# Selection products for the second attention's head stacks, key copies on ScalarE, and a new order of GpSimd's and SyncE's work

## The chip, the cores and the metric

The kernel runs on 1 core of one Trainium2 chip. The metric is the device time of one execution in microseconds (us). Engines are TensorE (PE in rows; PEld is its weight load), VectorE (DVE), ScalarE (ACT), GpSimd (POOL) and SyncE (SP), which issues DMAs.

## What is computed

Two transformer layers on x, 2 batches of 512 tokens by 128 features, with a context of 2 x 154 tokens. `_layernorm` has no weights.

```python
x = x + L0_xattn(_layernorm(x), ctx)   # linear attention with elu+1 features, then its own layer norm
x = x + L0_ffn(_layernorm(x))          # gated recurrence over the 2 batches as steps, tanh output
x = x + L1_xattn(_layernorm(x), ctx)   # softmax attention, 16 heads of 8 features, padding mask
x = x + L1_ffn(_layernorm(x))          # 8 experts, top 2, hidden 256
# L1_xattn:
Q = (q @ Wq + bq).reshape(Bc, Tq, H, HD).transpose(0, 2, 1, 3)
KV = (kv @ Wkv + bkv).reshape(Bc, Tk, 2, H, HD).transpose(2, 0, 3, 1, 4)
attn = softmax(where(mask, -inf, einsum('bhqd,bhkd->bhqk', Q, K) * HD ** -0.5))
out = einsum('bhqk,bhkd->bhqd', attn, V)   # then @ Wo + bo
```

## The kernel before

All data stay in SBUF; each engine runs one program in order, and the engines wait for one another by semaphores. Product accuracy near float32 comes from splitting an operand in a high part (type fp32r) and a low part, the rest after it.

**Layer 0** (to about 60 us). Context keys and values (L804, L808), layer norm of x on VectorE and ScalarE (`ln_apply`, `normalise`), turned by TensorE; queries (L820), key-value state (L827), `numerator(b)` (L833) and, after VectorE's `quotient(b)`, `project(b)` (L838), then VectorE's `residual(b)` (L1214) with its statistics. GpSimd computes the reciprocal roots (`rstd_of`, L467). The gates of the second layer part are L871 to L885, with tanh on ScalarE (L685).

**Second attention.** The 16 heads go in `HQ` = 4 stacks of `HG` = 4 heads for each batch, 8 stacks `m` in all. A stack's 97 score rows are three blocks of `QB` = 32 rows (4 heads x 8 features) and a row for the mask. For the keys block 0 and 1 are the high part and block 2 the low; for the queries block 0 and 2 high and block 1 low, so one product of 97 rows holds high x high, low x high and high x low. Before the change GpSimd builds for this the repeated weights `wq_r`, `wk_r` and the repeated identity `ident_r` (`three_blocks`, L485 to L490). The product with repeated weights (L861 for keys, L907 for queries, both float32, two passes) lays the stack out in PSUM three times; ScalarE copies all blocks rounded to fp32r (L671, L701); VectorE overwrites the low block with the rest (L1257, L1288). Biases are turned into the same layout (L854). GpSimd then writes the keys four times, for each head with the other heads' rows times 0 (`kz`, `kz_t`, L541 and L543).

For stack `m` TensorE makes 8 score products (`scores`, L919), VectorE takes the negated row maxima of each (L1298) and splits them in three bf16 parts (L1306 to L1309), TensorE turns them (`max_turn`, L928) and ScalarE copies them under the queries (L597). Then 5 units for each stack: transposed scores `st(u)` (L950), exp (L722) and, `LAG` = 4 units later, the product with the values (`pv`, L967 and L970). `ITEMS` (L383) is the order, written by hand, in which turns, queries, scores and maxima are put between units; `PER_UNIT` says how many go behind each, `ALONE` how many go before the first unit, and each item takes the next of a ring of PSUM banks (`BEFORE` waits for its last user).

**Experts** (from about 160 us): products of high and low parts of weights and activations. ScalarE rounds the weights (`weight_hi`, L604, 8 instructions) and GpSimd computes the rest (`weight_lo`, L478, 8 instructions); GpSimd also subtracts the first row of each expert's weights (L515) and builds the expert selectors `pick_e` (L556, L557) and the parts of the bias (L560 to L563).

SyncE issues the loads x, row constants, the weights of layer 0, of its gates, of layer 1, then the experts' three loads of 1 MB; ScalarE issues the context, its weights, the column constants and the mask (L590 to L593).

## Time and profile before

| | |
|---|---|
| time, median of 3 runs | 227.08 us (225.4 to 227.48) |
| the profiled execution | 226.56 us |
| its span, first to last instruction | 224.8 us |
| TensorE busy | 172.1 us (77%) |
| VectorE busy | 143.8 us (64%) |
| ScalarE busy | 99.9 us (44%) |
| GpSimd busy | 81.0 us (36%) |
| mean granted TensorE clock | 0.863 of full |

The profile is of one execution. Times in a timeline are us from the span's start. A line is `start, duration, engine, source line, operation, out<-in, shapes, count` and in brackets the engine's idle time before and what ended it.
### The profile page before, as it was taken

To read this page: it belongs to the slowest core of one execution; us is meant where nothing else is said; L and a number is where in the kernel's file an instruction comes from. 1 tells how busy PE (TensorE), PEld (TensorE's weight loads), DVE (VectorE), ACT (ScalarE), POOL (GpSimd) and SP (SyncE) were. 2 spreads that over 40 slices of the span, in tenths; PEclk is the share of its full clock that TensorE was granted. 3 is DMA by queue.
4 is the path that set the end of the run, shared out by engine and by line. 5 is a ranking of instruction groups with operands and counts; after the bars stand their busy time and mean duration, and the time that the engine had idled before them with its cause. 6 is when DMAs were issued, how large, how long until landed. Compare 5 with 4: busy or idle time off the path is not lost.

```text
span 224.8 us, 2308 instructions
## 1 busy us (share of the span) xinstructions
PE 172.1 (77%) x663; PEld 101.0 (45%) x663; DVE 143.8 (64%) x422; ACT 99.9 (44%) x184; POOL 81.0 (36%) x101
## 2 busy tenths in 40 slices
PE   0558983199518709889696978876899998999994
PEld 0334471144114207444244364433467674767682
DVE  5596899845386898756517375553468695656651
ACT  2135773551415105565424335652554635464551
POOL 7399453679149970000000000110334423342420
PEclk9995579679985755999766788996999999999999
DMA  6995000000000000000000000000000000000101
GB/s 188 315 274 180 1 0 1 0 4 0 0 1 0 0 0 0 0 0 0 3 0 0 0 0 0 4 0 0 0 3 0 1 0 0 3 0 0 47 1 47
DMA packets 4560, 6.04 MB, mean 27 GB/s; under 512 B 412, under 2 KB 3268, under 8 KB 4548
## 3 DMA queue, kind: packets, MB, share of 16 engines
q1 hardware_dynamic: 3984, 5.47, 7.9%
q10 hardware_dynamic: 564, 0.43, 0.7%
q8 instruction: 5, 0.08, 0.1%
q14 instruction: 7, 0.06, 0.1%
HBM read 5.37 MB, written 0.52 MB: 26 GB/s over the span
## 4 chain that ended last, share of the span: by engine, by line
PE 49%; DVE 35%; ACT 7%; issue 4%; DMA 3%; POOL 0%; ACTq 0%; DVEq 0%
DVE nmax L1298 6%; PE bank L967 4%; PE bank L907 4%; DVE stats L1111 3%; PE bank L871 3%; PE bank L919 3%; PE bank L1055 3%; DVE nm_part L1306 3%; DMA wc_s<-in_w_ctx 3%; PE bank L797 3%; PE bank L970 3%; PE bank L950 2%; PE bank L1057 2%; PE bank L1056 2%; PE bank L1040 2%
## 5 line engine op out<-in xcount | busy, mean ns | idle before, releaser
L467 POOL TENSOR_TENSOR rstd<-vare,m_half 128x4 f32<-128x4 f32 x10 | 10.9, 1092 | 80.6 <-DVE vare L1116 80.1
L569 POOL TENSOR_TENSOR pair<-early,pair 128x512 fp32r<-128x512 f32 x16 | 20.5, 1283 | 42.9 <-ACT pair L747 42.9
L1298 DVE TENSOR_REDUCE nmax<-bank 128x2 f32<-128x308 f32 x64 | 27.1, 471 | 12.0 <-PE bank L919 11.4
L1386 DVE SCALAR_TENSOR_TENSOR pair<-bank,pair 128x512 fp32r<-128x512 f32 x32 | 21.6, 689 | 19.6 <-ACT pair L754 19.5
L722 ACT ACTIVATE prob<-bank 128x512 f32<-128x512 f32 x40 | 23.4, 597 | 22.2 <-PE bank L950 21.9
L919 PE MATMUL bank<-pair,q_s 97*128 97x308 f32 x64 | 24.2, 441 | 5.9 <-DVE q_s L1288 3.7
L919 PEld LDWEIGHTS bank<-pair,q_s 97*128 97x128 f32 x64 | 13.8, 226 | 20.5 <-issue 7.1
L747 ACT ACTIVATE pair<-early 128x512 fp32r<-128x512 f32 x16 | 10.1, 632 | 23.9 <-DVE early L1382 23.9
L950 PE MATMUL bank<-q_s,pair 112*128 112x512 f32 x40 | 20.7, 530 | 0.0
L754 ACT ACTIVATE pair<-bank 128x512 fp32r<-128x512 f32 x32 | 18.7, 594 | 4.3 <-PE bank L1042 3.1
L797 PE MATMUL bank<-ident,a_n 128*128 128x128 f32 x40 | 8.5, 350 | 13.1 <-DVE a_n L1122 13.0
L797 PEld LDWEIGHTS bank<-ident,a_n 128*128 128x128 f32 x40 | 6.3, 182 | 18.3 <-issue 15.6
L1055 PE MATMUL bank<-pair,w_h 128*128 128x512 f32 x32 | 14.1, 441 | 0.0
L1040 PE MATMUL bank<-pair,w_h 128*128 128x512 f32 x32 | 13.5, 421 | 0.0
L1288 DVE SCALAR_TENSOR_TENSOR q_s<-bank,bias_q,q_s 32x512 fp32r<-32x512 f32 x8 | 6.0, 744 | 10.6 <-ACT q_s L701 10.5
L1042 PE MATMUL bank<-pair,w_l 128*128 128x512 f32 x32 | 12.7, 396 | 0.0
L1041 PE MATMUL bank<-pair,w_h 128*128 128x512 f32 x32 | 12.7, 396 | 0.0
L1057 PE MATMUL bank<-pair,w_h 128*128 128x512 f32 x32 | 12.7, 396 | 0.0
L1056 PE MATMUL bank<-pair,w_l 128*128 128x512 f32 x32 | 12.6, 395 | 0.0
L1382 DVE TENSOR_TENSOR early<-bank,q 128x512 f32<-128x512 f32 x16 | 10.9, 683 | 1.4 <-PE bank L1026 1.3
L701 ACT ACTIVATE q_s<-bank,bias_q 97x512 fp32r<-97x512 f32 x8 | 5.5, 688 | 13.8 <-PE bank L907 13.8
L907 PE MATMUL bank<-a_f,wq_r 128*97 128x512 f32 x16 | 11.0, 771 | 0.7 <-ACT a_f L597 0.7
(209 smaller groups left out, 353.7 us busy)
## 6 DMA issues: line engine op xcount, KB each, us to landing
w_s<-in_w SPq DMA_DIRECT2D x1, 1024.0 KB, 9.4
prob<-in_w SPq DMA_DIRECT2D x1, 1024.0 KB, 14.4
x_t<-in_x SPq DMA_DIRECT2D x2, 256.0 KB, 3.3
wf_s<-in_w_ffn SPq DMA_DIRECT2D x1, 512.0 KB, 8.5
row<-in_rows SPq DMA_DIRECT2D x1, 452.0 KB, 7.8
wc_s<-in_w_ctx ACTq DMA_DIRECT2D x1, 256.0 KB, 6.4
out_x<-x SPq DMA_DIRECT2D x1, 256.0 KB, 2.0
out_x<-x SPq DMA_DIRECT2D x2, 128.0 KB, 1.8
```

The lines of the kernel that those rows point to most:

```text
L569: pool.tensor_tensor(ec_l[:, n % NEC], ec[:, n % NEC], ec_h[:, n % NEC].bitcast(F32), ALU.subtract).then_inc(ec_lo, 1)
L722: nc.scalar.activation(prob[:, u % NPR], bank[ST[u % 3]][:], ACT.Exp).then_inc(prob_ready, 1)
L754: nc.scalar.activation(hid_h[:, g % NH], bank[RING[g % 4]][:], ACT.Relu).then_inc(hid_hi, 1)
L797: last = pe.transpose(dst[:, j * P:(j + 1) * P], src[:, j], ident[:])
L907: pe.matmul(item_bank("query", m)[0:ROWS_SCORE], wq_r[:, q], s_f[:, b], start=True, stop=True)\
L919: pe.matmul(item_bank("score", n)[:, 0:2 * TK].rearrange("p (g k) -> p g k", k=TK), q_s[0:ROWS_SCORE, b, q, j * P:(j + 1) * P], kz[0:ROWS_ ...
L950: pe.matmul(bank[ST[u % 3]][:], stack, q_s[0:ROWS_ALL, b, hq], start=True, stop=True).then_inc(st_mm, 1)
L1040: pe.matmul(o, wh, ec_h[:, n % NEC], start=True, stop=False)
L1055: pe.matmul(y, w2_h[:, e, c], hh, start=False, stop=False)
L1057: last = pe.matmul(y, w2_h[:, e, c], hl, start=False, stop=e == E - 1 and c == HC - 1)
L1298: dve.tensor_reduce(nmax[:, b, q, j, g:g + 2], item_bank("score", n)[:, 0:2 * TK].rearrange("p (h k) -> p h k", k=TK), AX.X, ALU.max, nega ...
L1386: dve.scalar_tensor_tensor(out=hid_l[:, g % NH], in0=bank[RING[g % 4]][:], scalar=0.0, in1=hid_h[:, g % NH].bitcast(F32), op0=ALU.max, op1 ...
```

## The change

1. **Queries.** One projection per batch (`project_q`, with the plain weights) replaces the product with repeated weights. ScalarE makes its high part, VectorE its low part, once for each batch. For each stack two products with a constant selection matrix `sel` (zeros and ones), one of the high and one of the low part, pick the three blocks (`select`); ScalarE copies the result with the row of ones added (`query_out`). The order `ITEMS` changes: both batches are projected first, and queries are picked two stacks ahead.
2. **Keys.** One product with the scaled weights early (in bank 5), its two parts, and 16 selection products of 160 columns between `numerator(0)` and `numerator(1)`, with three copies out on ScalarE. `kz` and `kz_t` are written by ScalarE, not GpSimd.
3. **GpSimd.** `three_blocks` gives way to four copies into `sel`. `pick_e` is written by one ScalarE copy from a small tile. The bias parts come earlier. `weight_lo` and the additions to `x2_bo` are held, to follow cell states and `nm_parts`. `weight_hi` moves behind the first step's gates on ScalarE.
4. **SyncE** waits for both context loads before row constants and everything behind them.
5. **VectorE.** `sel` is zeroed, `iota_f` and `head_of` come at the start.

```diff
@@ order of the second attention's items
-        ITEMS = [("turn", 0), ("query", 0), ("turn", 1), ("query", 1)] + [("score", n) for n in range(SPM)]
+        ITEMS = [("turn", 0), ("proj", 0), ("turn", 1), ("proj", 1), ("query", 0), ("query", 1)]
+        ITEMS += [("score", n) for n in range(SPM)] + [("query", 2), ("max", 0)]
         for m in range(1, NM):
             part = [("score", m * SPM + n) for n in range(SPM)]
-            if m + 1 < NM:
-                part.insert(0 if m == 1 else 4, ("query", m + 1))
-            part.insert(1 if m == 1 else 2, ("max", m - 1))
+            if m + 2 < NM:
+                part.append(("query", m + 2))
+            if m > 1:
+                part.insert(4, ("max", m - 1))
             ITEMS += part
-        ALONE = ITEMS.index(("max", 0)) + 4
+        ALONE = ITEMS.index(("max", 0)) + 6
@@ SyncE
+            sp.wait_ge(ld_ctx, 32)
             sp.dma_start(row[:], rows.partition_broadcast(P)).then_inc(ld_row, 16)
@@ GpSimd
-            three_blocks(ident_r, ident[:], 1.0)
+            pool.wait_ge(sel_zero, 1)
+            for k in SEL_ON:
+                pool.tensor_copy(sel[:, :, QB * k:QB * k + QB].rearrange("p q (d g) -> p q d g", g=HG),
+                                 ident[:].rearrange("p (d q g) -> p q d g", q=HQ, g=HG)).then_inc(sel_ready, 1)
...
-            for k in range(2, 8):
-                weight_lo(k)
+            for m in range(6):
+                pool.wait_ge(nm_parts, m + 1)
+                if m < 5:
+                    weight_lo(3 + m)
+                if m in (1, 5):
+                    add_rows(x2_bo, x2, R_BO1, m // 4, x2_bo_ready)
@@ ScalarE, behind uo_half and ahead of normalise(LN_R, 1)
+            for k, pairs in enumerate(K_PAIRS):
+                n = len(pairs) * TKP
+                copy_out(bank[K_BANK[k]][0:ROW_ONE, 0:n], k_flat[0:ROW_ONE, pairs[0] * TKP:pairs[0] * TKP + n],
+                         k_mm, k + 1, kf_ready)
...
+                nc.scalar.activation(kz[0:ROWS_ALL, :, :, g], k_f[0:ROWS_ALL], ACT.Copy, scale=own)\
+                  .then_inc(kz_ready, 1)
@@ ScalarE, gates
+                if step == 0:
+                    for k in range(8):
+                        weight_hi(k)
@@ TensorE
+            def select(out, windows, q, parts):
+                for k, (at, n) in enumerate(windows):
+                    mm = pe.matmul(out[0:n], sel[:, q, at:at + n], parts[:, k], start=k == 0, stop=k == 1)
+                return mm
             numerator(0)
+            pe.wait_ge(v1_ready, NB)
+            pe.wait_ge(sel_ready, len(SEL_ON))
+            for k, pairs in enumerate(K_PAIRS):
+                for i in pairs:
+                    q, b = divmod(i, NB)
+                    c = i % 3 * TKP
+                    last = select(bank[K_BANK[k]][:, c:c + TKP], SEL_K, q, k_hl[:, :, b * TKP:b * TKP + TKP])
+                last.then_inc(k_mm, 1)
             numerator(1)
...
+            def project_q(b):
+                pe.wait_ge(s_f_ready, b + 1)
+                pe.matmul(item_bank("proj", b)[:], w3_s[:, 0:P], s_f[:, b], start=True, stop=True).then_inc(q1_mm, 1)
             def query(m):
-                pe.matmul(item_bank("query", m)[0:ROWS_SCORE], wq_r[:, q], s_f[:, b], start=True, stop=True)\
-                  .then_inc(q_mm, 1)
+                pe.wait_ge(q_lo, b + 1)
+                select(item_bank("query", m)[:], SEL_Q, q, q_hl[b]).then_inc(q_mm, 1)
@@ VectorE, start
+            dve.memset(sel[:].bitcast(F32), 0.0).then_inc(sel_zero, 1)
...
+            dve.tensor_copy(iota_f[:], iota_u[:])
+            link(dve.tensor_reduce(head_of[:], ident[:].rearrange("p (c g) -> p g c", g=HG), AX.X, ALU.add))
@@ VectorE, second attention
-            def query_lo(m):
+            def query_lo(b):
+                dve.wait_ge(q_hi, b + 1)
+                dve.scalar_tensor_tensor(out=q_hl[b][:, 1], in0=item_bank("proj", b)[:], scalar=col[:, C_BQ1:C_BQ1 + 1],
+                                         in1=q_hl[b][:, 0].bitcast(F32), op0=ALU.add, op1=ALU.subtract)\
```

## Rows read from the trace of the kernel before

**Rows 1.** Windows: us, busy (x instructions) by engine, granted clock, DMA share, GB/s.
```profile
24.00:26.00 2.00, 2.00 (x4) 0.73 (x4) 1.66 (x3) 1.26 (x6) 0.95 (x1) 0.50 0.00 0
75.00:85.00 10.00, 4.52 (x12) 2.12 (x13) 9.40 (x12) 1.13 (x2) 8.02 (x8) 0.52 0.00 0
85.00:160.00 75.00, 61.13 (x269) 33.33 (x267) 42.85 (x147) 35.83 (x65) 1.73 (x3) 0.84 0.00 1
106.00:109.00 3.00, 1.61 (x7) 0.72 (x5) 2.64 (x7) 2.29 (x5) 0.00 (x0) 1.00 0.03 5
109.00:112.00 3.00, 2.35 (x13) 0.82 (x13) 1.22 (x5) 1.19 (x2) 0.00 (x0) 0.60 0.00 0
106.00:139.00 33.00, 27.24 (x106) 14.14 (x104) 17.38 (x50) 12.99 (x24) 0.00 (x0) 0.74 0.00 0
160.00:180.00 20.00, 19.95 (x97) 13.22 (x90) 13.08 (x33) 10.77 (x21) 8.90 (x8) 1.00 0.00 1
```

**Rows 2.** Timeline, before the first maxima are turned.
```profile
75.77 7.36 POOL L478 TENSOR_TENSOR w_l<-w_s,w_h 128x512 fp32r<-128x512 f32 x6
...
77.58 5.59 DVE L1306 CAST nm_part<-nmax 128x16 bf16<-128x16 f32 x1
...
83.94 0.58 PE L928 MATMUL bank<-ident_b,nm_part 128*16 128x128 bf16 x4 [5.48 <-DVE nm_part L1309]
```

**Rows 3.** Chain that ended last (start us, us, what), one stack's query.
```profile
97.66 0.88 PE bank L907 x2
...
99.28 0.75 DVE q_s L1288
100.08 0.41 PE bank L919
```

**Rows 4.** Waits of TensorE from 85 to 160 us: total us, times, longest.
```profile
PE bank L928 <- DVE nm_part L1309: 3.0, 3, 1.5
PE bank L919 <- DVE q_s L1288: 2.5, 4, 0.9
```

**Rows 5.** Chain that ended last, front and first residual.
```profile
1.46 6.39 DMA wc_s<-in_w_ctx
...
12.12 2.18 DVE a_n L1122 x4
...
30.82 0.69 DVE y_t L1214
```

**Rows 6.** Page, DMA issues: KB each, us from issue to landing.
```profile
row<-in_rows SPq DMA_DIRECT2D x1, 452.0 KB, 7.8
```

**Rows 7.** Groups by line: busy us, mean ns, idle before.
```profile
L1396 DVE CAST iota_f<-iota_u 128x8 f32<-128x8 uint32 x1 | 1.2, 1230 | 0.0
...
L1138 DVE MEMSET v_a<- 128x1024 f32 x1 | 0.9, 912 | 0.3 <-issue 0.3
```

**Rows 8.** Timeline, numerators and first projection.
```profile
24.05 3.77 PE L833 MATMUL bank<-q,kv 128*128 128x512 f32 x4
...
27.64 1.07 PE L838 MATMUL bank<-w_s,prob 128*128 128x128 f32 x8
```

**Rows 9.** Timeline of ScalarE: mask, weights' high parts, first residual, gates.
```profile
26.79 1.27 ACT L662 ACTIVATE q_s<-mask_u 1x1280 fp32r<-1x1280 uint8 x1
...
28.08 4.27 ACT L604 ACTIVATE w_h<-w_s 128x512 fp32r<-128x512 f32 x8
...
37.50 1.65 ACT L616 ACTIVATE y_t<-y_t,mean_rstd,rstd 128x128 f32<-128x128 f32 x4 [5.15 <-POOL mean_rstd L470]
...
55.26 0.69 ACT L685 ACTIVATE prob<-bank,gate 128x512 f32<-128x512 f32 x1 [4.70 <-PE bank L885]
```

**Rows 10.** Timeline, before the first maxima.
```profile
68.92 2.02 PE L907 MATMUL bank<-a_f,wq_r 128*97 128x512 f32 x2 [0.69 <-ACT a_f L597]
...
71.83 0.60 ACT L597 ACTIVATE a_f<-bank 128x512 f32<-128x512 f32 x1 [0.16 <-PE bank L797]
...
74.37 3.17 DVE L1298 TENSOR_REDUCE nmax<-bank 128x2 f32<-128x308 f32 x8
```

More of the change, by code:

```diff
@@ L375, in two_blocks @@
         XP = ((4, 5), (2, 3))
-        K_BANK = (3, 7, 4, 5)
+        K_BANK = (0, 2, 3)
+        K_PAIRS = [range(3 * k, min(3 * k + 3, HQ * NB)) for k in range(3)]
         OUT = ((0, slice(0, NJ), XP[0][1]), (1, slice(0, NJ // 2), XP[1][1]), (1, slice(NJ // 2, NJ), XP[0][0]))
@@ L515, in _ @@
                 pool.tensor_tensor(w1_s[:, s], w1_s[:, s], w1_first[:, s], ALU.subtract).then_inc(w1_based, 1)
-            for k in range(2):
-                weight_lo(k)
+            pool.wait_ge(w1_based, 4)
+            pool.wait_ge(ld_b2, 48)
+            link(pool.tensor_copy(b2_part[:, 0], b2_s[:]))
+            link(pool.tensor_tensor(b2_r[:], b2_s[:], b2_part[:, 0], ALU.subtract))
+            link(pool.tensor_copy(b2_part[:, 1], b2_r[:]))
+            pool.tensor_tensor(b2_part[:, 2], b2_r[:], b2_part[:, 1], ALU.subtract).then_inc(b2_ready, 1)
+            pool.wait_ge(b2_ready, 1)
             for b in range(NB):
@@ L523, in _ @@
             pool.wait_ge(v_pad, 1)
-            def second_values(b):
+            for b in range(NB):
                 pool.wait_ge(v1_ready, b + 1)
@@ L759, in _ @@
                     item(0)
-            for i in range(1, 4):
+            for i in range(1, FIRST):
                 item(i)
@@ L857, in _ @@
             project(1)
-            for q in range(HQ):
-                if q >= 2:
-                    pe.wait_ge(r_ready, q - 1)
-                pe.matmul(bank[K_BANK[q]][0:ROW_ONE, 0:NB * TKP], wk_r[:, q], ctx_t[:], start=True, stop=True)\
-                  .then_inc(k_mm, 1)
             pe.wait_ge(gate_c_ready, 1)
@@ L933, in wait_item @@
                 kind, m = ITEMS[i]
-                pe.wait_ge({"turn": s_f_ready, "query": q_lo, "score": max_taken, "max": nm_f_ready}[kind], m + 1)
+                pe.wait_ge({"turn": s_f_ready, "proj": q_lo, "query": q_ready, "score": max_taken,
+                            "max": nm_f_ready}[kind], m + 1)
             def item(i):
@@ L939, in item @@
                 kind, m = ITEMS[i]
-                {"turn": turn_in, "query": query, "score": scores, "max": max_turn}[kind](m)
+                {"turn": turn_in, "proj": project_q, "query": query, "score": scores, "max": max_turn}[kind](m)
             def st(u):
@@ L1251, in _ @@
                 ln_apply(LN_X1, b, x1, z_n, NJ_DVE).then_inc(z_ready, 1)
-            dve.wait_ge(bias_ready, 1)
-            for q in range(HQ):
-                rows = slice(2 * QB, 3 * QB)
-                dve.wait_ge(kf_ready, q + 2)
-                src = bank[K_BANK[q]][rows, 0:NB * TKP].rearrange("p (b k) -> p b k", b=NB)
-                dve.scalar_tensor_tensor(out=k_f[rows, :, q], in0=src, scalar=bias_k[rows, q:q + 1],
-                                         in1=k_f[rows, :, q].bitcast(F32), op0=ALU.add, op1=ALU.subtract)\
-                   .then_inc(k_lo, 1)
             for step in range(NB):
@@ L1402, in _ @@
                             maximum(m)
-                        elif kind == "query":
+                        elif kind == "proj":
                             query_lo(m)
```

184 lines of the change are left out of this document (91 added, 93 removed).

## Prediction

> **What bounds the kernel now.** The page's busy shares, in the table further up, show no engine full and TensorE the busiest at 77%. A table by stretches [rows 1] then shows two kinds of time. From 160 us on TensorE is busy all the time at full clock, so the tail, some 62 us of expert products, is bound by TensorE's work; the change adds no work to it. Before that TensorE waits, and pays twice: after a stretch in which it was little busy its granted clock falls to the lower level (1.2 of 2.4 GHz). From 75 to 85 us it is busy 4.52 of 10 us at clock 0.52. In the second attention a gap (106 to 109 us, busy 1.61 of 3) is followed by 3 us at 0.60; there are three such pairs, with gaps near 106, 118 and 130 us.
>
> The timeline names the largest wait [rows 2]: VectorE's cast of 16 columns (L1306) took 5.59 us. It began in a burst of six GpSimd subtractions (L478, 75.77 to 83.13 us) and ended as the burst did. TensorE's turning of the row maxima (L928), and behind it every score in order, waited until 83.94.
>
> The chain in the second attention [rows 3] shows the other wait. Each stack of four heads begins with a query product (0.88), a ScalarE copy, a VectorE subtraction (0.75) and only then its first scores: 100.08 - 97.66 = 2.42 us from product to score, on the path at five of the later stacks. The table of waits [rows 4] gives TensorE's idle time at that subtraction, 2.5 us in four waits, and at the maxima's parts 3.0 us in three.
>
> **The change part by part: the front.** SyncE now waits for the context weights before it issues the row constants and all later loads. These weights land at 1.46 + 6.39 = 7.85 us [rows 5]. With only 0.92 MB ahead (x 512 KB, context 154, weights 256) I estimate 5.3 us. Row constants (452 KB) landed 7.8 us after issue, beside other loads [rows 6]; from a queue to themselves I estimate 9 to 9.5 us, at worst 5.4 + 7.8 = 13.2. VectorE needs them at 12.12 us, where its normalisation starts [rows 5]. By then it has gained a memset of 1028 columns (0.91 us for 1024 [rows 7]), while the weights come 2.5 us earlier.
>
> The cast to `iota_f` moves from an idle place to the front. It took 1.23 us beside GpSimd work [rows 7]; it will meet GpSimd's four copies into `sel` (about 0.5 us each, as the blocks they replace). Rows 2 say that such a cast waits for the end of a burst, so it ends near 4.1 us, 1.6 after its turn. Half of that is free, since VectorE waited for x and for the weights there. Front: -2.5 + 0.9 (memset) + 0.3 (what the idle time leaves of the cast) = -1.3 at the normalisation, between -2.6 (the memset and the cast both in idle time) and +1.1 (constants at 13.2).
>
> The Trainium skill (SBUF — State Buffer, Who interferes with whom) says that a cast and a GpSimd instruction exclude each other and that the loser waits for the whole instruction. It speaks against this placement as well. It would charge the rest of one copy, some 0.5 us, and move the front to about -2.4; the trace shows waiting for six instructions in a row, and the measurement decides.
>
> Then the keys' selection: 16 products of 160 columns between `numerator(0)` and `numerator(1)`. Four passes of 512 columns take 3.77 us, mostly at the lower clock [rows 8], 0.94 each, so 160 columns 0.29; at full clock 8 passes of 128 columns take 1.07, so 160 take 0.17. Sixteen: 4.7 or 2.7 us. The clock was 0.50 at 24 to 26 [rows 1], and the eight fast passes begin at 27.64, so it rose between; I take 3.9. `numerator(0)` ends at about 24.05 + 2 x 0.9 - 1.3 = 24.5, and ScalarE's copies of the values are done before; so the selection ends at 28.4, `numerator(1)` (0.9 to 1.8) at 29.7, `project(0)` (1.07 to 2.0) at 31.0. Before, `residual(0)` began at 30.82 [rows 5]; now at 31.0. What the front gains the selection takes: term A = 0, bounds -0.6 (full clock throughout) and +1.4 (lower clock throughout). If a short product of this type cost a fixed 0.53 us (a little over half of a 512-column pass at the lower clock, and three times what its columns come to at full clock), the selection would take 8.5 us: A = +4.
>
> The removed key products, bias turnings and the four VectorE key subtractions stood beside a VectorE chain from 31 to 43 us, and save nothing. The keys' eight masked copies go from GpSimd to ScalarE. The only row of that width on ScalarE is the mask copy, 1280 columns in 1.27 us [rows 9]; with 0.4 for each tail 4 x 1.67 = 6.7 us, from 29.3 (after three copies out of PSUM) to 36.0. Behind them is queued `normalise(LN_R, 1)`, which began at 37.50 after 5.15 us idle: hidden, with 1.5 to spare. `weight_hi`'s eight copies (4.27 us) move into ScalarE's gap of 4.70 us before the tanh at 55.26 [rows 9]: hidden, 0.4 to spare. GpSimd's first low parts (1.25 each, a sixth of the burst) start with the first cell state and end 2.5 us later; VectorE's next work follows the tanh at 55.26. The key product (1.1 us) and its two parts (0.5 each) lie before 18 us beside VectorE's and ScalarE's own waits: 0.
>
> **Before the first maxima.** Before, one query product at 68.92, a copy, a subtraction and a second query give the first maximum at 74.37 [rows 10]. Now the projection takes the query product's time, but the second batch's turn and projection stand before the first selection in TensorE's order: the second turned copy is ready at 71.83 + 0.60 = 72.43, projection(1) to 73.4, selections(0) and (1) to 75.1, ScalarE's copy to 75.05, first maximum 75.6, +1.2 (bounds +0.7 and +3, all at half clock). Eight maxima (3.2) and four part instructions (0.8) end at 79.7. GpSimd now holds its low parts until after these parts, one or two instructions (1.25, or 2.5) for each stack, and the next stack's eight maxima cover them. So the 5.4 us of stall go: maxima turned at 79.8 instead of 83.94. Term B = -4.1, bounds -4.7 and -2.3. If the cover fails each stack loses at most 1.3 us.
>
> **The second attention.** Queries are picked up to two stacks ahead, as one copy on ScalarE; VectorE's subtraction (six times 0.74) is gone. TensorE's own work is the same: two passes either way. From TensorE's waits the sure part is the 2.5 us of rows 4; of the 3.0 us at the maxima's parts, which start late because their scores do, I count 1. The larger part is the clock. From 106 to 139 us [rows 1] TensorE is busy 27.24 us at a mean clock of 0.74: 20.2 us of full-speed work in 33 us elapsed. With a tenth of waits left, keeping the clock would save some 11 us. The gaps at 106, 118 and 130 all lie in the query chain, but maxima and parts are in them too; I count one of the three dips, about 1.5 us. Term C = -2.5 - 1 - 1.5 = -5.0, bounds -2.5 and -11.
>
> **Sum.** 0 - 4.1 - 5.0 = -9.1 us. The profiled execution has a span of 224.8 and a time of 226.56, 0.52 under the median of 227.08; 226.56 - 9.1 = 217.5, beside the median 218.0. I predict 218.0, a ratio of 0.960. Its own range is 214 to 221.5.
>
> **Rivals.**
> (1) The clock holds: most of the dips vanish, C = -9 to -11, time 212 to 214. For it: every dip follows a gap in which a query chain lies. Against: the gaps at 118 and 130 also hold waits for maxima, and the stretch from 142 to 154, where the gating chain runs, stays. The Trainium skill (TensorE: Matmul & The Clock Gate, HAM oscillation) has it that waits between groups of products throttle the array anew each time; by that rule a queue without the query waits keeps the clock, which is this rival. The trace agrees so far, with 0.60 behind the gap at 106 us.
> (2) The selection of the keys becomes the bound: A = +4, ScalarE's masked copies end near 41 us and delay `normalise(LN_R, 1)` by the same amount. Time 222. For it: no row shows a short product of this type. Against: from 128 to 512 columns the durations of rows 8 follow the columns.
> (3) Only the stall goes: the query chain was covered by TensorE's other work, C = 0 to -1; time 222 to 223. For it: TensorE is busy 61.13 of 75 us from 85 to 160 [rows 1]. Against: the 2.5 us of direct waits.
> (4) Not faster: the order with two batches' projections first and with the maxima's turn after four scores makes new gaps, and the clock is at the lower level for most of the attention. Each us of full-speed work done there costs one more. Work from 85 to 160 us is 61.13 x 0.84 = 51 us, about 10 of it now at the lower level (61 - 51). Nine more us of it cancel the whole gain; time 226 to 230. That needs the lower level in 19 of the 51 us of work, twice as much as now. Against: the new order takes waits out of TensorE's queue.
> That the change does nothing is no case: the burst from 75.77 on is taken apart.
>
> **How the numbers follow.** Forecast 0.55, rival (1) 0.17, (2) 0.09, (3) 0.11, (4) 0.08. The range 212.5 to 223 takes in rivals (1) to (3) nearly whole and leaves out about two tenths, most of it (4) and the outer ends of C. A measurement of this kernel tells 1%, 2.3 us, from no change. Faster by over 1% (under 224.8) is all but (4) and a little of (3): 0.90; same 0.06; slower 0.04.
>
> **What would show it.** The cast at the first maxima at 0.2 us and the first turned maxima near 80 us show B. VectorE's normalisation at about 10.8 us, and `residual(0)` at 31, show A; the cast to `iota_f` far over 0.2 us would show the burst rule. Products of the selection near 0.17 to 0.29 us against 0.5 decide rival (2). TensorE's clock from 100 to 135 us, and no wait of the scores for queries, show C. The prediction is wrong if ScalarE's copies run past the second residual's statistics, or if the clock in the attention is lower than before.

## The result and the profile after

The changed kernel takes 211.15 us (median of 4 runs, 209.87 to 211.63), the kernel before, on the same chip, 226.3 us. The ratio is 0.932, with an interval of 0.925 to 0.939. The forecast was 218.0 us, a ratio of 0.960, with a range down to 212.5. The direction was right, and the gain was larger by nearly 7 us than forecast: the time lies below the range.

Executions of one kernel differ by some per cent, and the profiled one is at times a slow one: 220.19 us for a_step (median 215.38), 216.14 for b_spread_order (214.18), 215.96 for a_dup_sel (214.08), 209.0 for a_pool_late (206.59), 214.26 for a_no_hold (212.16). The profiled execution of the changed kernel took 210.78 us, with a span of 208.9 us where before had 224.8. Five moments that both kernels have cut the span into stages. They are read from the timelines: `residual(0)` begins; the first maxima are turned; batch 0's projected sum is added into `x3`; the first expert product begins; the end.

| stage | before, us | after, us | difference |
|---|---|---|---|
| start to `residual(0)` | 30.82 | 31.12 | +0.3 |
| to the first maxima turned | 53.12 | 48.64 | -4.5 |
| to `x3` of batch 0 | 58.97 | 43.57 | -15.4 |
| to the first expert product | 18.56 | 21.00 | +2.4 |
| to the end | 63.3 | 64.6 | +1.3 |
| span | 224.8 | 208.9 | -15.9 |

The first two rows are terms A and B of the prediction (0 and -4.1), the third is term C (-5.0). The last row is no effect of the change: over all sixteen executions profiled for this document that stage takes either 63.2 to 63.4 us (ten, a second execution of the changed kernel among them) or 64.6 to 64.7 (six, b_spread_order among them, a variant of the kernel before). The windows of the third stage, before and after, show which engine did what (columns as in [rows 1]: us, then busy time by engine in the order TensorE, weight loads, VectorE, ScalarE, GpSimd, then the granted clock):

```profile
83.94:142.91 58.97, 49.64 (x207) 28.00 (x208) 34.69 (x100) 28.02 (x49) 0.00 (x0) 0.81 0.00 1
```

```profile
79.76:123.33 43.57, 39.84 (x207) 25.08 (x208) 29.88 (x93) 27.82 (x49) 8.83 (x7) 0.93 0.00 1
123.33:144.33 21.00, 18.00 (x71) 7.74 (x69) 9.70 (x50) 8.45 (x17) 3.00 (x4) 0.66 0.00 1
```

TensorE was busy 84% of the stage before, and 91% after. Its busy time times the clock is the work at full speed: 49.64 x 0.81 = 40.2 us before, 39.84 x 0.93 = 37.1 us after. So the 15.4 us of this stage are made up, rounded, of 3.1 us less work, 5.6 us less waiting (58.97 - 49.64 = 9.3 us idle before, 3.7 after) and 6.6 us less time lost to the clock (busy time less work: 9.4 us before, 2.8 after). The second line is the stage behind it, where half of the clock was lost for much of the time (0.66). The page of the kernel after shows the clock there too, at 5 tenths in the 26th to 28th of its 40 slices (130.6 to 146 us):

```profile
PE 165.1 (79%) x669; PEld 99.2 (47%) x669; DVE 130.4 (62%) x414; ACT 109.0 (52%) x196; POOL 65.3 (31%) x87
...
PEclk9985588558997695799999999555999999999999
```

**The first maxima.** The timeline of after, which answers to [rows 2] and [rows 10]:

```profile
75.60 3.17 DVE L1329 TENSOR_REDUCE nmax<-bank 128x2 f32<-128x308 f32 x8 [0.31 <-PE bank L956]
...
78.81 0.18 DVE L1337 CAST nm_part<-nmax 128x16 bf16<-128x16 f32 x1
...
79.69 1.27 POOL L495 TENSOR_TENSOR w_l<-w_s,w_h 128x512 fp32r<-128x512 f32 x1 [11.79 <-DVE nm_part L1340]
...
79.76 0.48 PE L965 MATMUL bank<-ident_b,nm_part 128*16 128x128 bf16 x3 [1.38 <-DVE nm_part L1340]
```

The cast took 0.18 us where it had taken 5.59, GpSimd's low part begins behind the four part instructions, and the turn comes at 79.76.

**One stack's query.** The chain that ended last, of after, answers to [rows 3]:

```profile
87.84 0.29 PE bank L956 x2
88.13 0.47 PE bank L875 x2
88.59 0.23 PE bank L988
88.82 0.29 PE bank L956 x2
```

The selection (L875) stands among other products as one more piece of TensorE's work, and no copy or subtraction of a query follows it on the chain. The pair takes 0.47 us, where the query product took 0.88 in [rows 3].

**The front.** The timeline of after, for [rows 5, 8, 9]:

```profile
2.69 0.26 DVE L1180 CAST iota_f<-iota_u 128x8 f32<-128x8 uint32 x1
...
9.82 3.80 DVE L1161 SCALAR_TENSOR_TENSOR a_n<-x_t,mv,rstd 128x128 f32<-128x128 f32 x4
...
25.43 2.99 PE L875 MATMUL bank<-q_late,sel 128*96 128x160 f32 x16
...
27.13 3.34 DVE L1232 RECIPROCAL q_m<-q_e 128x512 f32<-128x512 f32 x1
...
31.12 0.68 DVE L1260 TENSOR_TENSOR y_t<-bank,y_t 128x512 f32<-128x512 f32 x1
```

The row constants landed in 4.0 us, against 7.8 in [rows 6].

**The chain by line.** The profile also sums the chain that ended last over a stretch. First before, from 84 to 143 us, then after, from 80 to 123:

```profile
by line: DVE nmax L1298 17.2%; PE bank L967 12.3%; PE bank L919 12.1%; PE bank L907 8.3%; PE bank L950 7.6%; PE bank L970 7.3%; DVE q_s L1288 6.3%; PE bank L928 6.2%; ACT q_s L701 5.9%; PE bank L987 3.2%; issue 3.0%; PE bank L996 1.9%; DVE 
```

```profile
by line: PE bank L956 20.5%; PE bank L988 13.6%; DVE nmax L1329 11.8%; PE bank L1005 11.6%; PE bank L1008 8.0%; issue 6.6%; PE bank L965 6.1%; PE bank L875 4.1%; PE bank L1025 2.7%; PE bank L1034 2.2%; ACT q_s L726 1.7%; ACT prob L749 1.5%;
```

Before, a stack's query (product L907, copy L701, subtraction L1288) is 8.3 + 5.9 + 6.3 = 20.5% of 59 us, 12.1 us. After, selection and copy are 4.1 + 1.7 = 5.8% of 43 us, 2.5 us. The difference in this view is 9.6 us; the prediction did not read it. It is a share of a chain and not yet a gain: what the gain is, the experiments have to show.

### The profile page after: what moved, and what is told of

It is laid out like the page before. It is cut to its first block, busy times and chain, and to the rows that moved or that the text cites. A ratio compares the mean times of both kernels' runs of the same rounds, so it can differ in the third digit from the quotient of the medians.

```text
span 208.9 us, 2327 instructions
## 1 busy us (share of the span) xinstructions
PE 165.1 (79%) x669; PEld 99.2 (47%) x669; DVE 130.4 (62%) x414; ACT 109.0 (52%) x196; POOL 65.3 (31%) x87
## 4 chain that ended last, share of the span: by engine, by line
PE 60%; DVE 27%; ACT 5%; issue 4%; DMA 1%; POOL 0%; DVEq 0%; ACTq 0%
PE bank L956 4%; PE bank L1094 4%; DVE nmax L1329 4%; DVE stats L1150 4%; PE bank L1079 4%; PE bank L1008 3%; PE bank L1080 3%; PE bank L906 3%; PE bank L988 3%; PE bank L1081 3%; PE bank L1005 3%; PE bank L1096 3%; PE bank L1095 3%; PE bank L824 3%; DVE a_n L1161 3%
## 5 line engine op out<-in xcount | busy, mean ns | idle before, releaser
L569 POOL TENSOR_TENSOR pair<-early,pair 128x512 fp32r<-128x512 f32 x16 | 20.5, 1283 | 46.5 <-ACT pair L774 46.5
L956 PE MATMUL bank<-pair,q_s 97*128 97x308 f32 x64 | 20.4, 388 | 2.4 <-DVE nmax L1329 1.3
L495 POOL TENSOR_TENSOR w_l<-w_s,w_h 128x512 fp32r<-128x512 f32 x8 | 10.2, 1275 | 35.2 <-DVE nm_part L1340 26.4
L988 PE MATMUL bank<-q_s,pair 112*128 112x512 f32 x40 | 18.8, 482 | 0.1
L956 PEld LDWEIGHTS bank<-pair,q_s 97*128 97x128 f32 x64 | 12.9, 211 | 12.0 <-DVE nmax L1329 6.1
L824 PEld LDWEIGHTS bank<-ident,a_n 128*128 128x128 f32 x40 | 5.9, 174 | 23.1 <-issue 20.5
L1079 PE MATMUL bank<-pair,w_h 128*128 128x512 f32 x32 | 14.4, 449 | 0.0
L1094 PE MATMUL bank<-pair,w_h 128*128 128x512 f32 x32 | 14.1, 440 | 0.0
L1080 PE MATMUL bank<-pair,w_h 128*128 128x512 f32 x32 | 13.0, 407 | 0.0
L1096 PE MATMUL bank<-pair,w_h 128*128 128x512 f32 x32 | 12.6, 395 | 0.0
L1005 PE MATMUL bank<-prob,v_a 128*32 128x512 f32 x64 | 10.3, 719 | 0.0
L1008 PE MATMUL bank<-prob,v_b 128*128 128x512 f32 x16 | 10.1, 718 | 0.0
## 6 DMA issues: line engine op xcount, KB each, us to landing
prob<-in_w SPq DMA_DIRECT2D x1, 1024.0 KB, 12.4
```

Source lines behind the costliest of these rows:

```text
L569: pool.tensor_tensor(ec_l[:, n % NEC], ec[:, n % NEC], ec_h[:, n % NEC].bitcast(F32), ALU.subtract).then_inc(ec_lo, 1)
L824: last = pe.transpose(dst[:, j * P:(j + 1) * P], src[:, j], ident[:])
L956: pe.matmul(item_bank("score", n)[:, 0:2 * TK].rearrange("p (g k) -> p g k", k=TK), q_s[0:ROWS_SCORE, b, q, j * P:(j + 1) * P], kz[0:ROWS_ ...
L988: pe.matmul(bank[ST[u % 3]][:], stack, q_s[0:ROWS_ALL, b, hq], start=True, stop=True).then_inc(st_mm, 1)
L1079: pe.matmul(o, wh, ec_h[:, n % NEC], start=True, stop=False)
L1080: pe.matmul(o, wh, ec_l[:, n % NEC], start=False, stop=False)
```

## The experiments

The theory after the result: in the second attention VectorE serves the scores' maxima and the queries' subtraction in one program, in order. While a query product and ScalarE's copy run, VectorE stands before its subtraction, and the maxima behind it wait, with the score banks that they would free. The rival: TensorE's clock is the cause, and each gap in TensorE's queue costs what the lower level makes of the work behind it. A second rival: TensorE itself has less to do.

Each experiment was timed beside the kernel before. "Stage" is that from the first turned maxima to `x3` of batch 0, in the profiled execution.

### The burst alone: b_spread

```diff
-            for k in range(2, 8):
-                weight_lo(k)
+            for m in range(6):
+                pool.wait_ge(nm_parts, m + 1)
+                weight_lo(2 + m)
```

> The kernel before, with one edit: GpSimd's last six low parts of the expert weights each wait for one stack's maxima parts, as in the changed kernel, in place of one burst. It measures term B by itself. Both theories expect the first maxima to be turned near 79.5 us instead of 83.9, the cast at 0.2 us instead of 5.6, and 221.5 to 222.5 us. If the stall was also what upset the clock later, the three dips near 110, 121 and 133 us vanish too and the time is 216 or less.

Measured: 219.6 us, ratio 0.980 (0.963 to 0.996). The cast is 0.18 us. From the first maximum to the turn it takes 4.16 us instead of 9.57, here and in every later kernel: 5.4 us less. The stage:

```profile
82.90:138.53 55.63, 45.81 (x207) 26.45 (x208) 34.91 (x99) 28.60 (x50) 7.57 (x6) 0.88 0.00 1
```

Busy time fell by 3.8 us at the same full-speed work (45.81 x 0.88 = 40.3), and the stage by 3.3. This is not the clock right behind the stall: up to the fifth turned maxima the stage is 2.0 us longer here than before (27.73 against 25.71 us), and behind it 5.4 us shorter, where the clock was 0.74 before and is 0.94 now.

```profile
109.65:142.91 33.26, 28.04 (x114) 15.14 (x115) 15.72 (x48) 13.01 (x23) 0.00 (x0) 0.74 0.00 0
```

```profile
110.63:138.53 27.90, 22.22 (x114) 12.70 (x115) 15.68 (x47) 12.94 (x23) 2.47 (x2) 0.94 0.00 1
```

Whether these 3.3 us come from the edit or from where the clock's dips fell in one execution is not shown. The other 12 us remain.

### The order on top of it: b_spread_order

```diff
+        ITEMS += [("query", 2), ("max", 0)]
         for m in range(1, NM):
             part = [("score", m * SPM + n) for n in range(SPM)]
-            if m + 1 < NM:
-                part.insert(0 if m == 1 else 4, ("query", m + 1))
-            part.insert(1 if m == 1 else 2, ("max", m - 1))
+            if m + 2 < NM:
+                part.append(("query", m + 2))
+            if m > 1:
+                part.insert(4, ("max", m - 1))
...
```

> The kernel before with the spread low parts and the new order of items (queries two stacks ahead, maxima turned after four scores), but the old query products with repeated weights and VectorE's subtraction for each stack. Theory order: what was missing from the prediction comes from the look-ahead alone, since it takes the chain product, copy, subtraction, score out of every stack; 211 to 214 us, clock at full from 90 to 130 us. Rival selection: the picked stacks matter, because VectorE's 0.74 us per stack is still ahead of maxima; 217 to 221 us.

Measured: 214.18 us, ratio 0.947 (0.924 to 0.970). The stage went from 55.63 to 46.82 us, with VectorE's subtraction still there:

```profile
81.89:128.71 46.82, 41.84 (x207) 24.11 (x208) 34.41 (x100) 27.86 (x49) 7.58 (x6) 0.96 0.00 1
```

VectorE's waits for ScalarE's copy of a query say why. First the kernel before (83 to 143 us), then this one (81 to 129 us); columns: total us, times, longest:

```profile
DVE nmax L1298 <- PE bank L919: 11.4, 8, 3.1
DVE q_s L1288 <- ACT q_s L701: 8.0, 5, 3.5
```

```profile
DVE nmax L1301 <- PE bank L922: 5.2, 7, 1.0
...
DVE q_s L1291 <- ACT q_s L704: 1.2, 1, 1.2
```

Asked for two stacks ahead, a query is there when VectorE comes to it. TensorE's own wait for the subtraction is 2.5 us in both. What went is VectorE's standing, 8.0 to 1.2 us, and its waits for scores, 8.4 to 5.2. (In b_spread, which differs from this run by the order alone, the two waits are 8.0 and 8.4 us; the 11.4 of before hold the wait behind the burst too.)

### Idle products in the waits: b_spread_fill

```diff
+            def fill(to, n):
+                pe.wait_ge(w_hi, 8)
+                for _ in range(n):
+                    pe.matmul(to, w1_h[:, 0, 0:P], w1_h[:, 0:2].rearrange("p e h -> p (e h)"), start=True, stop=True)
...
                 if i == 0:
+                    if m >= 2:
+                        fill(item_bank("score", n)[:], 2)
                     pe.wait_ge(q_lo, m + 1)
```

> The kernel before with the spread low parts, and with two idle products of 512 columns (weights by weights, written to the score's bank and overwritten) ahead of the wait for a stack's queries, from the third stack on. They do no work of the kernel; the query chain is as long as before. Theory clock: the missing gain was the granted clock, so filling TensorE's gaps keeps it at full through 110, 121 and 133 us and the time falls to 215 to 218 us. Theory latency: the missing gain was the wait itself, so the fillers bring nothing, 221.5 to 224 us.

Measured: 220.82 us, ratio 0.983 (0.971 to 0.995), the same as b_spread within the intervals. The stage is 56.83 us, clock 0.88, as in b_spread: the idle products did not raise the clock, so this run shows that they bring nothing, and not what a higher clock would bring. From 90 us on the clock was high already in b_spread (0.94, and 0.93 with the idle products), and the stage still took 12 us more than in the changed kernel. What part of it is left at full clock, the windows under "The subtraction put back" show.

### The subtraction left out: b_spread_nolow

b_spread without VectorE's subtraction in each stack; the low part of the queries is left out of the scores, which now wait for ScalarE's copy.

```diff
-                        elif kind == "query":
-                            query_lo(m)
...
-                    pe.wait_ge(q_lo, m + 1)
+                    pe.wait_ge(q_hi, m + 1)
...
```

> The kernel before with the spread low parts, and without VectorE's subtraction for each stack of queries: the low part of the queries is left out of the scores (the block holds the rounded value again), so the output is not the reference's. TensorE's work and the order of items are as before. Theory chain: VectorE's 0.74 us, and VectorE standing still in its program until ScalarE has copied, hold the maxima; without them most of what the new order brought comes too, 213 to 216 us. Rival work: TensorE's query product is what costs, then 218 to 220 us (b_spread: 219.6).

Measured: 211.45 us, ratio 0.944 (0.936 to 0.951). In the old order, one instruction of 0.75 us fewer per stack takes 7.9 us from the stage. TensorE's work hardly changed (41.08 x 0.96 = 39.4 by this line, 40.3 in b_spread). Its idle time fell from 9.8 to 6.6 us, and the rest is busy time, 45.81 to 41.08, nearly all of it by the clock (0.88 to 0.96):

```profile
80.64:128.35 47.71, 41.08 (x207) 24.17 (x208) 30.11 (x93) 27.73 (x49) 7.58 (x6) 0.96 0.00 1
```

### The changed kernel in the old order: a_old_order

The edit of b_spread_order, undone in the changed kernel (queries one stack ahead, the turn after one or two scores).

> The changed kernel with the old order of items: each query is picked one stack ahead, and maxima are turned after two scores. Everything else is as changed. Theory order: the query chain (selection, copy, score, some 1.6 us instead of 2.4) is back in every stack and the dips with it, 217 to 221 us. Rival selection: the time stays at 211 to 213 us.

Measured: 213.23 us, ratio 0.954 (0.942 to 0.966); stage 44.61 us. Without the subtraction the order is worth little: the changed kernel's own stage was 43.57 us, and 45.09 in a second execution (a_again, below). This is the rival's time, and not the 217 to 221 us of the theory. Whether the 2% between the ratios 0.954 and 0.932 is real stays open, since they come from different comparisons.

### The subtraction put back: a_step and a_old_step

An instruction of the same size on VectorE (32x512), between ScalarE's copy and the scores; it changes no value. a_step has the new order, a_old_step the old one.

```diff
+            def query_step(m):
+                b, q = divmod(m, HQ)
+                rows = slice(QB, 2 * QB)
+                dve.wait_ge(q_ready, m + 1)
+                dve.scalar_tensor_tensor(out=q_s[rows, b, q], in0=item_bank("query", m)[rows],
+                                         scalar=one_row[rows], in1=q_s[rows, b, q].bitcast(F32),
+                                         op0=ALU.add, op1=ALU.max).then_inc(q_step, 1)
...
-                    pe.wait_ge(q_ready, m + 1)
+                    pe.wait_ge(q_step, m + 1)
```

> The changed kernel, with a VectorE step of the old size (32 rows, 512 columns) put back between ScalarE's copy of a stack's queries and its scores; it rewrites the same values. Order two stacks ahead as changed. Theory chain (VectorE's step, by its place in VectorE's program, costs about 1 us per stack, less where the look-ahead covers it): 2 to 4 us slower than the changed kernel. Theory work of TensorE: at most 1 us slower.

> The same VectorE step put back, with the old order of items (one stack ahead): the cheap picked products stay, the old chain is complete. Theory chain: this loses nearly all of what b_spread_nolow gained over b_spread (8 us): 217 to 220 us, 6 us or so above the changed kernel with the old order (213.2). Theory work: the products are still cheap, so 213 to 215 us.

Measured: a_step 215.38 us, ratio 0.957 (0.953 to 0.962), stage 47.58. a_old_step 222.74 us, ratio 0.985 (0.974 to 0.995), stage 54.59:

```profile
84.59:139.18 54.59, 45.06 (x207) 26.39 (x208) 34.62 (x99) 27.86 (x49) 8.81 (x7) 0.86 0.00 1
```

a_step lies in the theory's range; a_old_step lost more than the 217 to 220 us expected. With the step in the old order nearly all that the stage gained over b_spread (55.63 us) is gone, though picking, projection, copies and low parts are those of the changed kernel. The four corners of the stage, in us (where two values stand, the first is of the kernel before with the spread low parts, the second of the changed kernel, with selection products and all its other edits):

| | old order, one ahead | new order, two ahead |
|---|---|---|
| with a VectorE step per stack | 55.63 / 54.59 | 46.82 / 47.58 |
| without it | 47.71 / 44.61 | - / 43.57, 45.09 in a_again |

Either edit alone takes 7 to 10 us, the two together 9.5 to 12. They remove the same standing, so their gains don't add up.

The clock differs between these executions. From the third to the sixth turned maxima, three stacks, it doesn't: TensorE had its full clock there in all of these runs but one. The windows of b_spread, b_spread_nolow, b_spread_order and after:

```profile
96.46:119.53 23.07, 17.54 (x78) 9.16 (x78) 14.62 (x41) 13.05 (x23) 4.12 (x4) 1.00 0.00 1
```

```profile
90.56:109.81 19.25, 16.66 (x78) 9.13 (x78) 12.41 (x38) 12.72 (x23) 4.13 (x4) 1.00 0.00 1
```

```profile
95.14:113.00 17.86, 15.51 (x76) 8.75 (x75) 14.08 (x39) 11.99 (x22) 3.82 (x3) 1.00 0.00 1
```

```profile
91.84:107.63 15.79, 14.34 (x76) 8.63 (x76) 11.57 (x36) 11.89 (x22) 3.85 (x3) 1.00 0.00 1
```

| three stacks, us | old order, one ahead | new order, two ahead |
|---|---|---|
| with a VectorE step per stack | 23.07 / 23.26 (clock 0.93) | 17.86 / 17.70 |
| without it | 19.25 / 17.86 | - / 15.79, 15.79 in a_again |

So at full clock in both, leaving the step out is worth 3.8 us in three stacks (23.07 to 19.25), the new order 5.2 (to 17.86), and both with the cheaper products 7.3 (to 15.79). The clock can't be the cause of that part. It is the cause of the rest in this sense only: in both runs that took the standing away from b_spread the stage's clock rose from 0.88 to 0.96, with no edit aimed at it. How much of that rise is the edit, and how much is where the dips fell in one execution, is open (after 0.93, a_again 0.89).

### The selection made twice: a_dup_sel

```diff
+                select(item_bank("query", m)[:], SEL_Q, q, q_hl[b])
                 select(item_bank("query", m)[:], SEL_Q, q, q_hl[b]).then_inc(q_mm, 1)
```

> The changed kernel with each stack's pair of selection products made twice (same result): TensorE's work for a stack's queries is then 0.92 us at full clock, as the 0.88 of the old product; the chain and VectorE's work stay as changed. Theory work: part of what the prediction missed is the 0.42 us of TensorE's time per stack that fp32r products of 512 columns save, in a stage where TensorE is busy nine tenths: 3 to 4 us slower than the changed kernel, 214 to 215. Rival latency: the stage is bound by waits, under 1.5 us slower.

Measured: 214.08 us, ratio 0.942 (0.931 to 0.952), beside 0.932 for the changed kernel: no clear difference. The stage is 44.72 us, within what the changed kernel itself shows. Doubling adds some 0.46 us for each of the stacks picked within it: the work at full speed is 41.49 x 0.96 = 39.8 us, 2.8 more than the 37.1 of after. TensorE's waits took little of that (3.2 us idle, against 3.7 in after and 3.5 in a_again); the clock, 0.96 against 0.93 and 0.89, happened to be higher. So this run does not decide between its two theories. The better measure is the first column of the two tables: with the step in place the cheaper products bring 1.0 us (55.63 to 54.59), and nothing in the three stacks (23.07 and 23.26); without it 3.1 (47.71 to 44.61), and 1.4 in the three stacks at full clock (19.25 to 17.86), near the 3 x 0.41 us that three query products save.

### The changed kernel once more, and idle products behind the stage: a_again and a_fill

> The changed kernel itself, once more, as the level for the other runs of this call: 210.5 to 212 us by every theory.

Measured: 212.23 us beside 224.59 for the kernel before. Its span was 208.6 us, but cut otherwise: `residual(0)` at 32.10, maxima turned at 83.34, `x3` at 128.43, first expert product at 145.38. It reached `x3` 5 us later than the first execution and made it good behind it (this stretch, and 1.4 us in the last stage):

```profile
128.43:145.38 16.95, 12.40 (x71) 5.75 (x69) 9.53 (x50) 8.19 (x16) 3.00 (x4) 1.00 0.00 1
```

The same 71 products took 16.95 us at full clock here and 21.00 at 0.66 above. In the sixteen kernels and executions seen this stretch takes 16.9 to 21.0 us, by where the clock's low stretches fall. The +2.4 us of the first table is such a difference, and no effect of the change.

a_fill puts two or three of the idle products above ahead of three waits of batch 0 behind the stage (the inputs of T_PROJ, T_IN and T_COMB):

```diff
                 elif piece == T_PROJ:
+                    if b == 0:
+                        fill(second[:], 2)
...
                 elif piece == T_COMB:
+                    if b == 0:
+                        fill(first[:], 3)
```

> The changed kernel with idle products (weights by weights into a free bank) in three waits of the first batch's tail: two of 512 columns before the turned attention output, two before the normalised input, three before the combination weights. They do no work of the kernel. In the changed kernel TensorE's clock is at half from 130 to 147 us, behind these waits. Theory clock: filled waits keep it at full, 3.5 to 5 us faster than the changed kernel, 206.5 to 208. Rival: the clock falls anyway or the fillers delay the chain, 211 to 213.

Measured: 210.59 us, ratio 0.938 (0.928 to 0.949): no difference. The clock fell all the same, later and for less long than in after (in a_again, without idle products, it did not fall there at all):

```profile
131.00:135.00 4.00, 3.17 (x16) 2.23 (x16) 1.29 (x11) 2.06 (x4) 0.51 (x1) 0.84 0.01 2
135.00:139.00 4.00, 4.00 (x16) 1.36 (x15) 2.68 (x20) 1.18 (x3) 0.00 (x0) 0.50 0.00 0
```

### GpSimd's additions held back: a_pool_late, a_pool_hold, a_fill_pool

In the changed kernel the normalisation took 3.80 us, where [rows 5] had 2.18. GpSimd's additions ran beside it:

```profile
9.40 2.54 POOL L499 TENSOR_TENSOR x_beta<-x_t,row 128x512 f32<-128x512 f32 x2
12.16 1.31 POOL L499 TENSOR_TENSOR y_t<-a_n,row 128x512 f32<-128x512 f32 x1 [0.23 <-DVE a_n L1161]
```

```diff
             pool.wait_ge(ld_row, 16)
+            pool.wait_ge(v0_ready, NB)
             for b in range(NB):
                 pool.wait_ge(ld_x[b], 16)
                 add_rows(x_beta, x_t, R_BETA, b, x_beta_ready)
```

> The changed kernel with GpSimd's four row additions held until VectorE has made both batches' context values. In the changed kernel VectorE's first normalisation takes 3.80 us beside these additions, in the kernel before 2.18, and the cast-like step at L1211 takes 1.06. Theory port: free of GpSimd the normalisation takes 1.4 to 1.6 us and the front ends 2 us earlier: residual(0) at 29 us, 208.5 to 209.5 us. Rival: something else (row constants, products of context) is due next and the front ends at most 0.5 us earlier, 210.5 to 212.

> The changed kernel with GpSimd's additions into x_beta and y_t held until after VectorE's first normalisation, once more, beside the kernel without SyncE's wait on the same chip. The port theory: the normalisation takes 1.1 us instead of 3.8, residual(0) begins near 26.5, the time is 206 to 208 (ratio 0.92). The rival, that the first run of it was chance: 211 to 212.

Measured: 206.59 us, ratio 0.920 (0.911 to 0.929), and 205.72 us, ratio 0.914 (0.896 to 0.931), in two comparisons. The changed kernel itself was in neither comparison; its nearest kin on the same chips, a_fill and a_no_hold, took 210.59 and 212.16 us, so the edit is worth 2 to 3%. The timeline of the second:

```profile
10.18 1.14 DVE L1162 SCALAR_TENSOR_TENSOR a_n<-x_t,mv,rstd 128x128 f32<-128x128 f32 x4 [0.39 <-DMA row<-in_rows]
...
11.75 0.29 DVE L1212 TENSOR_SCALAR early<-early 128x256 f32<-128x256 f32 x1
...
14.21 2.49 POOL L499 TENSOR_TENSOR x_beta<-x_t,row 128x512 f32<-128x512 f32 x2 [4.91 <-issue]
...
26.57 0.68 DVE L1261 TENSOR_TENSOR y_t<-bank,y_t 128x512 f32<-128x512 f32 x1
```

The four normalisations take 1.14 us, the next but two on VectorE 0.29 instead of 1.06, and `residual(0)` begins at 26.57 instead of 31.12: 4.6 us. 3.4 us of it are these two rows; between 9 and 26 us the granted clock was also 1.00 instead of 0.65. The Trainium skill (SBUF — State Buffer, Who interferes with whom) says that a VectorE instruction with two inputs in SBUF contends with a GpSimd instruction that reads SBUF. The trace agrees, with 3.80 us beside the additions and 1.14 without.

> The changed kernel with both later edits: GpSimd's row additions held until the context values are made (206.6 us alone) and idle products in three waits of the first batch's tail (210.6 alone). If the granted clock behind the tail can be held, 203.5 to 205.5 us; if the fillers bring nothing, 206 to 207.5.

Measured, with a_fill's idle products as well: 204.3 us, ratio 0.903 (0.893 to 0.912), the fastest of all; on the same chip the changed kernel took 212.23 (a_again). Since a_fill alone brought nothing that can be told and the intervals of a_fill_pool and a_pool_hold overlap, the gain over the changed kernel is put down to the held additions; what the idle products add is open.

### The loads not held: a_no_hold

```diff
-            sp.wait_ge(ld_ctx, 32)
             sp.dma_start(row[:], rows.partition_broadcast(P)).then_inc(ld_row, 16)
```

> The changed kernel without SyncE's wait for the context weights before it issues the row constants. My theory: the wait orders the front's transfers, so without it the weights and x land later beside 2.6 MB more; the normalisation still starts when the constants have landed, and the front moves by no more than 1 us either way; time 211 to 213, a ratio to the kernel before of 0.94, as the changed kernel's. The rival: the wait carries part of the surplus over my forecast; then the weights land 2.5 us later, residual(0) begins 2 us later than 31.1, near 33, and the time is 213.5 to 215.

Measured: 212.16 us, ratio 0.935 (0.917 to 0.952). The row constants take 7.0 us from issue instead of 4.0, the context weights 6.4 instead of 3.8:

```profile
11.69 3.66 DVE L1160 SCALAR_TENSOR_TENSOR a_n<-x_t,mv,rstd 128x128 f32<-128x128 f32 x4
```

The normalisation begins 1.9 us later than in after and `residual(0)`, at 32.87, 1.8 later (0.8 later than in a_again, 0.5 later than in a_fill, which has the changed kernel's front). The front came out near the rival's 33, the time in my own range. The held loads are worth 0.5 to 1.8 us at this point of the trace; the time can't tell it.

## Why the prediction was right and wrong

**Term C, the step that failed: "From TensorE's waits the sure part is the 2.5 us of rows 4."** TensorE's waits of [rows 4] name only what TensorE waited for last, and are the same 2.5 us in b_spread_order, where the stage is 8.8 us shorter. The query chain's cost lay in VectorE's program: 8.0 us of standing before five subtractions and six subtractions of 0.74, 12.4 us together, and while VectorE stood, the maxima of scores that were done stood behind it. The chain by line had it too, with 12.1 us. Both rows lay in the trace of before. The runs put the removal of the step and the new order, with the cheaper products, at 10.5 to 12 us (55.63 to 45.09 and 43.57), 7.3 of them in three stacks at full clock. Term by term, by the windows of before and after: my 2.5 + 1 us for waits measured 5.6, my 1.5 us for the clock 6.6, and the work, which I put at nothing, 3.1. Waits and clock can't be kept apart by cause: both fell when VectorE's standing went.

**"TensorE's own work is the same: two passes either way."** Wrong. A stack's selection pair takes 0.47 us at full clock, the float32 query product 0.88. Worth 0 to 1.0 us while the chain sets the stage, and up to 3.1 once it doesn't.

**The clock.** I took the clock for the larger part, and bounded C by it at -11. By the windows it is the largest of the three parts, with 6.6 us, but it followed: taking VectorE's step away raised it from 0.88 to 0.96 by itself. So rival (1), whose time of 212 to 214 was near, was right that most of the dips go with the query waits (from the second turn on, at 86 us, to `x3` the clock of after is at full), and left out what the standing cost at full clock and the work that was saved. A run in which the clock alone is held is missing: the idle products of b_spread_fill left it at 0.88. By the rule that the prediction set beside it (the Trainium skill, TensorE: Matmul & The Clock Gate, HAM oscillation), waits between groups of products throttle the array anew. The trace agrees that the dips follow waits (0.60 behind the gap at 106 us). That filling the waits would hold the clock did not come out here: 0.88 with and without idle products.

**Term B was right in size and cause.** The stall gave back 5.4 us in each of the kernels without the burst (9.57 to 4.16 us from first maximum to turn). The longer way to the first maximum was forecast at +1.2 us, and measured 1.1 in the first two executions (from the first projection to the first maximum: 5.45 before, 6.55 and 6.56 after), and 2.6 in a_no_hold (8.0; 8.0 in a_old_order too), within the bound of +3. That the turn came at 79.76 where 79.8 was forecast is partly luck. In a_again it came at 83.34, because `residual(0)` was 1 us later and the stretch behind it, at a clock of 0.78 instead of 0.86 from 45 to 69 us, another 2.6. This stretch, from `residual(0)` to the first projection, took 38.1 us in before and 37.9 in after, and 39.9 to 40.6 in all fourteen other executions, with the old front and the new: the first table's pair is a fair one, but neither of the two is typical. The prediction also misread its row: the cast did not wait for six instructions. It began 1.8 us into the burst, in the second of them, and waited for the rest of that one and for four more.

**Term A was right as a sum, by errors that cancelled.** Forecast 31.0, measured 31.12. But:
- The constants had landed by 9.40 us, when GpSimd's additions, which wait for them, began; the normalisation came after a memset, at 9.82 instead of 10.8 us. It took 3.80 us instead of the 2.18 that I left as it was: I moved it to where GpSimd's additions begin at the same event, and did not ask what runs beside it there.
- The `iota_f` cast took 0.26 us, not 1.6 beyond its turn. GpSimd's four copies took 1.00 us together, 0.25 each where I took 0.5, and ended at 3.15 us; the cast ended at 2.95. So the rule of the burst, taken from the 5.59 us at the maxima, did not hold here. The Trainium skill's rule beside it (SBUF — State Buffer, Who interferes with whom), a wait for the running instruction alone, fits this cast and not that one. What tells the two apart is open.
- The keys' selection took 2.99 us, 0.19 for each product, within my 0.17 to 0.29. It did not move the front at all. The second batch's reciprocal (27.13, 3.34 us) and quotient stand ahead of `residual(0)` in VectorE's program, and set its start; the selection ended at 28.42 beside them. It was so before: `project(0)` ended at 27.64 + 1.07 = 28.71 us [rows 8], 2.1 us ahead of `residual(0)`. So the path of term A, selection, `numerator(1)`, `project(0)`, `residual(0)`, was the wrong one, and that the sum met the measured time is luck. Rival (2) fell.

**Hidden as forecast:** ScalarE's masked copies end at 35.8 us (forecast 36.0), and `normalise(LN_R, 1)` begins at 37.66 after 1.85 us of idle time (forecast 1.5); `weight_hi`'s copies (4.25 us) leave 0.55 us before the tanh (forecast 0.4).

**Rivals (3) and (4)** fell. (3) took the chain for covered because TensorE was busy 61 of 75 us; much of that busy time was at the lower level. (4) needed more of the work at the lower level, and there was less.

## What to carry to other kernels

When an engine serves two chains in one program, read that engine's own waits and its lines on the chain that ended last before you size the gain of taking a step away; the waits of the bound engine show only the last of the causes. Here a 0.75 us instruction cost 8 to 10 us per eight stacks because other work stood behind it, and asking for its input one stack earlier saved nearly as much as removing it. To keep the clock out of such a comparison, read it in a stretch where the granted clock is the same in both. When a step is moved forward, look up what the other engine starts on the same event: holding GpSimd's additions back by 5 us gave 2 to 3% more.

## What the runs showed of the hardware

- Selection products of 512 columns in the reduced float32 type, with 97 weight columns, take 0.23 us each on the chain at full clock; the float32 product of the same size takes 0.88, as two instructions of 0.44. At 160 columns, with a weight load of 96 columns ahead of each, they took 0.19 us each, at a mean clock of 0.62.
- Four VectorE instructions with two SBUF inputs of 128x128 take 1.14 us alone, and 3.80, 4.26 and 3.66 us beside GpSimd's 128x512 additions (after, a_again, a_no_hold).
- The granted clock's low stretches fall at different places in executions of the same kernel. From 45 to 69 us it was 0.86 or 0.78, and one stretch of 71 products took 16.95 or 21.00 us, with spans of 208.6 and 208.9. One profile's stage is good to some 2 us here. Three stacks at full clock took 15.79 us in both.
